# Attention output weights in two TensorE products a tile instead of three, with the output's low half stored beneath its high half

## What is computed

```
ln = layernorm(latents, ln_l_g, ln_l_b)
q = ln @ Wq.T
kv = jnp.concatenate([xn @ Wkv.T, ln @ Wlkv.T], axis=1)
...
attn = jax.nn.softmax(attn, axis=-1)
out = jnp.einsum('bhij,bhjd->bhid', attn, v)
out = out.transpose(0, 2, 1, 3).reshape(b, m, INNER)
return out @ Wo.T + bo
```

## Time and profile before

| | us |
|---|---|
| median of 3 runs | 823.86 (823.17 to 824.24) |
| the profiled execution | 826.39 |
| its span (first to last instruction) | 824.5 |
| PE busy | 760.7 (92%) |
| VectorE busy | 528.5 (64%) |
| ScalarE busy | 399.1 (48%) |
| GpSimd busy | 319.7 (39%) |

### The profile page before, as it was taken

The page is one execution under the profiler, slowest core; times in us unless marked ns, Lnnn a source line. Parts: engine busy times, 40 slices in busy tenths (PEclk is TensorE's granted clock), DMA queues, the critical chain, the costliest instruction groups (busy, mean ns, idle before and its releaser), DMA issues.

```text
span 824.5 us, 12845 instructions
## 1 busy us (share of the span) xinstructions
PE 760.7 (92%) x4881; PEld 621.4 (75%) x4881; DVE 528.5 (64%) x1163; ACT 399.1 (48%) x699; POOL 319.7 (39%) x281
## 2 busy tenths in 40 slices
PE   8889989999999999999999899983799999999996
PEld 7755546656755554679889888882788999999996
DVE  7767875773677683357455498975746656667552
ACT  3655634573465344563462244433034765557551
POOL 5502001200301022066361053334235878787783
PEclk9999999999999999999999999995699999999998
DMA  7000000000000100100030201121212444544532
GB/s 186 1 0 1 1 0 1 1 0 1 1 1 2 51 4 0 52 1 3 1 98 1 103 2 52 52 77 39 103 34 78 132 119 147 129 116 110 142 33 32
DMA packets 21509, 39.31 MB, mean 48 GB/s; under 512 B 4913, under 2 KB 16905, under 8 KB 19145
## 3 DMA queue, kind: packets, MB, share of 16 engines
q1 hardware_dynamic: 14793, 30.07, 11.1%
q0 software_dynamic: 6656, 8.43, 5.9%
HBM read 29.96 MB, written 8.40 MB: 47 GB/s over the span
## 4 chain that ended last, share of the span: by engine, by line
PE 56%; DVE 15%; ACT 4%; issue 3%; POOL 3%; another core or an unknown queue 0%; DVEq 0%; ACTq 0%
PE ps L481 18%; PE ps L650 8%; PE ps L1173 5%; PE ps L1176 5%; PE ps L754 5%; PE ps L671 2%; PE ps L672 2%; PE ps L612 2%; PE ps L475 1%; DVE sm L1613 1%; DVE rep L1807 1%; PE ps L1096 1%; DVE Pb L1617 1%; DVE sm L1622 1%; POOL out_dram L2724 1%
## 5 line engine op out<-in xcount | busy, mean ns | idle before, releaser
L650 PE MATMUL ps<-PT,VA 128*65 128x512 f32 (+1 forms) x288 | 147.5, 594 | 2.8 <-ACT PT L2116 2.5
L2116 ACT ACTIVATE PT<-ps 128x512 f32<-128x512 f32 x128 | 76.0, 594 | 62.0 <-PE ps L672 61.7
L481 PE MATMUL ps<-GT,wh 128*128 128x258 f32 (+1 forms) x768 | 94.6, 284 | 0.4 <-DVE GT L1905 0.4
L481 PEld LDWEIGHTS ps<-GT,wh 128*128 128x128 f32 x768 | 92.7, 189 | 0.6 <-DVE GT L1905 0.6
L2724 POOL DMA_INDIRECT out_dram<-ye,idx x40 | 67.2, 1679 | 19.9 <-issue 10.9
L2410 ACT ACTIVATE het<-ps,b1e 128x514 f32<-128x514 f32 x64 | 44.1, 689 | 61.4 <-PE ps L481 53.7
L1940 DVE TENSOR_TENSOR he<-het,he 128x514 fp32r<-128x514 f32 x64 | 45.6, 713 | 40.2 <-ACT he L1969 38.2
L671 PE MATMUL ps<-QA,KA 128*128 128x512 f32 x144 | 67.5, 468 | 0.8 <-ACT QB L1969 0.8
L2460 POOL TENSOR_TENSOR rs<-rs,half 128x4 f32<-128x4 f32 (+2 forms) x19 | 18.2, 956 | 123.5 <-DVE rs L1214 95.6
L612 PE MATMUL ps<-KA,QA 128*128 128x368 f32 x192 | 59.2, 414 | 4.4 <-DVE x L1422 2.1
L2602 POOL DMA_INDIRECT gt<-y_dram,idx x40 | 46.3, 1158 | 43.3 <-DVE gate L1895 33.5
(11 more groups left out here) (291 smaller groups left out, 1654.2 us busy)
## 6 DMA issues: line engine op xcount, KB each, us to landing
wr<-in_w1e_dram SPq DMA_DIRECT2D x8, 1024.0 KB, 5.0
wr<-in_w2e_dram SPq DMA_DIRECT2D x8, 1024.0 KB
x<-in_x_dram SPq DMA_DIRECT2D x4, 512.0 KB, 6.2
w<-in_w_dram SPq DMA_DIRECT2D x2, 1024.0 KB, 4.7
y_dram<-yr SPq DMA_DIRECT2D x3, 512.0 KB, 3.0
out_dram<-x SPq DMA_DIRECT2D x3, 512.0 KB, 4.1
b2r<-in_b2r_dram SPq DMA_DIRECT2D x8, 128.0 KB, 3.3
gt<-y_dram,idx POOLq DMA_INDIRECT x40
```

The lines of the kernel that those rows point to most:

```text
L481: op = pe.matmul(o, l, r, start=n == 0, stop=n == len(calls) - 1)
L650: pe.matmul(bank[6 + hf][0:65, :], VA[b][0:K, kt, h, :], PT[u % 4][0:K, :], start=kt == 0, stop=kt == 8).then_inc(p_pv, 1)
L2116: a.activation(PT[u % 4][0:K, :], bank[4 + u % 2][0:K, :], ACT.Exp, bias=0.0 if K == 128 else mcol[:, b:b + 1]).then_inc(a_exp, 1)
```

## The change

OT[0] gets 128 rows: rows 0 to 63 hold the output's high half, rows 64 to 127 its low half. wo[0] holds the high half of the weights in rows 0 to 63 and once more in rows 64 to 127, so that one matmul of 128 rows makes high by high and low by high. OT[1] is the companion: rows 0 to 63 the high half again, row 64 and row 65 the denominator's high half, row 96 its low half, zeros between; wo[1] holds the low half of the weights in rows 0 to 64 and the high row of bias and denominator in rows 65 and 96. Each tile then takes a matmul of 97 rows and one of 128.

For that, ScalarE makes two copies of a half instead of one and VectorE two subtractions instead of one; VA has two columns of ones; GpSimd clears 64 rows of wo[1] and of OT[1]; SyncE copies the rows of wo by three DMAs. The handling of a head's second half moves from its end to unit 0 of the next head, and `lnf` on GpSimd waits for VectorE's v_lr ahead of `add_row`.

```diff
-                three(bank[m][:, 0:258], [((OT[0][:, c], OT[1][:, c]), (wo[0][:, h, :], wo[1][:, h, :]))]).then_inc(p_wo, 1)
+                pe.matmul(bank[m][:, 0:258], OT[1][0:97, c], wo[1][0:97, h, :], start=True, stop=False)
+                pe.matmul(bank[m][:, 0:258], OT[0][:, c], wo[0][:, h, :], start=False, stop=True).then_inc(p_wo, 1)
...
             def attention(hi):
-                def ot(hf):
+                def ot(hi, hf):
                     qc = slice(512 * hf, 512 * hf + 512)
                     v.wait_ge(a_ot, 2 * hi + hf + 1)
-                    v.tensor_tensor(OT[1][:, qc], bank[6 + hf][0:65, :], f(OT[0][:, qc]), ALU.subtract).then_inc(v_ot, 1)
+                    v.tensor_tensor(OT[0][64:128, qc], bank[6 + hf][0:64, :], f(OT[0][0:64, qc]), ALU.subtract)
+                    v.tensor_tensor(OT[1][96:97, qc], bank[6 + hf][64:65, :], f(OT[1][64:65, qc]), ALU.subtract).then_inc(v_ot, 1)
...
+                    if hi and u == 0:
+                        ot(hi - 1, 1)
                     if hi and u % 2 and u < 16:
                         wo_tile(hi - 1, u // 2)
                     yield
-                ot(1)
+                if hi == 7:
+                    ot(hi, 1)
...
-                        a.wait_ge(g_wlo, 3)
-                    copy(OT[0][:, qc], bank[6 + hf][0:65, :]).then_inc(a_ot, 1)
+                        a.wait_ge(g_init, 7)
+                    copy(OT[0][0:64, qc], bank[6 + hf][0:64, :])
+                    copy(OT[1][0:66, qc], bank[6 + hf][0:66, :]).then_inc(a_ot, 1)
...
                     a.activation(PT[u % 4][0:K, :], bank[4 + u % 2][0:K, :], ACT.Exp,
                                  bias=0.0 if K == 128 else mcol[:, b:b + 1]).then_inc(a_exp, 1)
+                    if hi and u == 0:
+                        ot(hi - 1, 1)
                     if u == 9:
-                        ot(0)
+                        ot(hi, 0)
...
                 g_.wait_ge(v_z, 4 + g + 1)
+                if g % 2 == 0:
+                    g_.wait_ge(v_lr, g // 2 + 1)
                 add_row(g)
...
             low(wv[1], wv_in, wv[0], 2)
+            g_.wait_ge(g_wlo, 2)
+            step(g_.memset(f(wo[1][64:128, :, :]), 0.0))
+            settle()
             step(g_.memset(wo_in[:, :, 256:258], 0.0))
...
             low(wqk[1][:, :, 256:512], wqk_in[1], wqk[0][:, :, 256:512], 4)
+            g_.wait_ge(g_wlo, 4)
+            g_.memset(f(OT[1][64:128, :]), 0.0).then_inc(g_init, 1)
+            g_.wait_ge(g_init, 7)
             proj(1)
...
+            sp.wait_ge(g_wlo, 3)
+            for p in (65, 96):
+                sp.dma_start(f(wo[1][p:p + 1, :, :]), f(wo[0][64:65, :, :])).then_inc(d_rows, 16)
+            sp.wait_ge(d_rows, 96)
+            sp.dma_start(f(wo[0][64:128, :, :]), f(wo[0][0:64, :, :])).then_inc(d_rows, 16)
```

More of the change, by code:

```diff
@@ L162, in build @@
         wo_at = RA.at
-        wo = [RA(f"wo{i}", [65, H0, 258], F32R)[:, :, :] for i in range(2)]
+        wo = [RA(f"wo{i}", [128, H0, 258], F32R)[:, :, :] for i in range(2)]
         qa_at = RA.at
@@ L168, in build @@
         KB = RA("KB", [65, H0, NK], F32R)
-        VA = [RA(f"VA{i}", [128, 9, H0, 65]) for i in range(2)]
+        VA = [RA(f"VA{i}", [128, 9, H0, 66]) for i in range(2)]
         gg = RA("gg", [128, 3])
@@ L178, in build @@
         ot_at = RA.at
-        OT = [RA(f"OT{j}", [65, S], F32R) for j in range(2)]
+        OT = [RA(f"OT{j}", [128, S], F32R) for j in range(2)]
         wo_in = Arena(ot_at)("wo_in", [65, H0, 258])[:, :, :]
@@ L631, in wo_tile @@
                 if hi == 0 and qt == 0:
-                    pe.wait_ge(a_whi, 3)
                     pe.wait_ge(g_wlo, 3)
-                three(bank[m][:, 0:258], [((OT[0][:, c], OT[1][:, c]), (wo[0][:, h, :], wo[1][:, h, :]))]).then_inc(p_wo, 1)
+                    pe.wait_ge(d_rows, 112)
+                pe.matmul(bank[m][:, 0:258], OT[1][0:97, c], wo[1][0:97, h, :], start=True, stop=False)
+                pe.matmul(bank[m][:, 0:258], OT[0][:, c], wo[0][:, h, :], start=False, stop=True).then_inc(p_wo, 1)
                 busy[m] = (v_x, 8 * hi + qt + 1)
@@ L649, in pv @@
                         pe.wait_ge(a_vc, 2 * b + 2)
-                    pe.matmul(bank[6 + hf][0:65, :], VA[b][0:K, kt, h, :], PT[u % 4][0:K, :], start=kt == 0,
+                    pe.matmul(bank[6 + hf][0:66, :], VA[b][0:K, kt, h, :], PT[u % 4][0:K, :], start=kt == 0,
                               stop=kt == 8).then_inc(p_pv, 1)
@@ L2333, in scalar_program @@
             a.wait_ge(g_wo, 1)
-            halved(wo[0], wo_in, (d_rows, 64))
+            halved(wo[0][0:65, :, :], wo_in, (d_rows, 64))
             values(0, 2, 6)
@@ L2617, in gpsimd_program @@
             for va in VA:
-                g_.memset(va[:, :, :, 64:65], 1.0).then_inc(g_init, 1)
+                g_.memset(va[:, :, :, 64:66], 1.0).then_inc(g_init, 1)
             g_.wait_ge(g_init, 3)
@@ L2635, in gpsimd_program @@
             root_c(0)
-            low(wo[1], wo_in, wo[0], 3)
+            low(wo[1][0:65, :, :], wo_in, wo[0][0:65, :, :], 3)
             for i in range(2):
```

## The result

| | before | after |
|---|---|---|
| median | 823.51 | 834.68 |
| all executions | 822.88 to 824.24 | 833.60 to 834.94 |
| ratio | | 1.0137 (1.0122 to 1.0153) |
| the profiled execution | 826.39 | 833.60 |
| its span | 824.5 | 831.8 |

The account below looks back on a forecast made before the run. TensorE, busy 92% of the span, was taken as the bound. The terms -6.2 - 1.7 + 6.9 + 4.5 + 0.2 gave +3.7 us on 823.86, so 827.5 us, with a range of 821.0 to 831.5.

Parts of the forecast that it names:

- the two stall terms: Longer OT hand-overs in unit 9, +6.9 us, and at the borders of the heads, +4.5 us.
- products: Output tiles on TensorE: 192 matmuls become 128, and 52 of the 64 removed count at 0.119 us each, -6.2 us.
- clock: No term; a different clock granted at the start was named among what could overturn the sum.
- v_lr: Head 6: GpSimd's add to x waits for VectorE's L1466 and TensorE's gap goes, -1.7 us; bounds 0 and -2.1.
- unit 9: Second copy and subtraction lengthen the chain by 1.1 us, paid in six heads, 0.3 in head 7: +6.9; bounds +3.3, +8.
- the borders of the heads: Second half handled behind the next head's exp(0) and two reductions, so bank 7 and VectorE are late: +4.5; bounds 0, +8.
- the start: GpSimd's clearing of wo[1] rows stretches one VectorE cast, +0.2 us; bounds 0 and +1.0.
- A: Rival: TensorE's queued matmuls make good what the small engines lose, so products decide: -9.1, 814.8 us; chance 0.07.
- B: Rival: the one-row subtraction is nearly free, unit 9 costs 3.0 and borders 2.2: -2.3, 821.6 us; chance 0.10.
- C: Rival: the borders cost nothing, since exp(0) goes first and bank 7 has slack: -0.8, 823.1 us; chance 0.18.
- D: Rival: delays carry on as bank 2 passes on late, each of 11 places half as much again: +5.5, 833 us; chance 0.15.
- The cost of the second subtraction: In unit 9's chain on VectorE, one row by 512 was taken at 0.61 us; bounds 0.1 and 0.61.

Follow-up runs that it names:

- a_third: The changed kernel with the 97-row product of every output tile issued twice, 64 matmuls more; ratio to the kernel before 1.0197 (1.0175 to 1.0219).
- a_dma: The changed kernel with one copy and one subtraction a half, companion rows moved by SyncE's DMA, second half handled at the head's end; ratio to before 0.9919.
- b_1row: The kernel before plus a one-row subtraction of 512 behind each of the 16 subtractions, into a row nothing reads; ratio to before 1.0107 (1.0082 to 1.0131).
- b_copy2: The kernel before plus a second copy of 65x512 behind each of ScalarE's 16 copies, into a tile nothing reads; ratio to before 1.0038 (1.0023 to 1.0053).
- b_moved: The kernel before with only the second half's handling moved into the next head's unit 0; ratio to before 0.9999 (0.9985 to 1.0013).
- b_vlr: The kernel before with only GpSimd's wait for v_lr ahead of the two adds to x; ratio to before 0.9960 (0.9949 to 0.9972).

## Why the prediction was wrong, step by step

The change was 7.5 us dearer than forecast. The steps that failed are the two stall terms, too small by 1.6 and 2.3 us, the products, put 1.6 too high, and the clock, which had no term and came to 3.0.

| step | forecast | measured |
|---|---|---|
| products | -6.2 | -4.6 (a_third: -4.1, by the medians -4.9) |
| v_lr | -1.7 | -1.7 |
| unit 9 | +6.9 | +8.5 |
| the borders of the heads | +4.5 | +6.8 |
| the clock | 0 | +3.0 |
| the start | +0.2 | -0.6 |

The measured terms are of the traces and sum to 11.4, against 11.5 for the last output product. The two middle rows come from a_dma, which has the same products, the same wait for v_lr and falls of the clock at the same two places as the changed kernel, but the short chains and the old place. Between the two the starts of the scores drift apart only in the units in which OT changes hands; elsewhere they keep step to 0.03 us. Units 10 and 11 of head 6, in a_dma and in the changed kernel:

```profile
295.40 0.40 PE L674 MATMUL ps<-QA,KA 128*128 128x512 f32 x1
...
297.71 0.40 PE L674 MATMUL ps<-QA,KA 128*128 128x512 f32 x1
```

```profile
306.82 0.39 PE L672 MATMUL ps<-QA,KA 128*128 128x512 f32 x1
...
310.44 0.40 PE L672 MATMUL ps<-QA,KA 128*128 128x512 f32 x1
```

2.31 us and 3.62: the chain costs 1.3 there. Place by place, forecast and measured:

| head | 0 | 1 | 2 | 3 | 4 | 5 | 6 | 7 | sum |
|---|---|---|---|---|---|---|---|---|---|
| unit 9, forecast | 1.1 | 1.1 | 1.1 | 0 | 1.1 | 1.1 | 1.1 | 0.3 | 6.9 |
| unit 9, measured | 1.30 | 1.25 | 1.25 | 0.36 | 1.12 | 1.30 | 1.30 | 0.66 | 8.5 |
| border into this head, forecast | | 0.5 | 0.8 | 0.5 | 0 | 0.5 | 0.7 | 1.5 | 4.5 |
| border into this head, measured | | 0.78 | 1.15 | 0.81 | 0.16 | 0.84 | 1.14 | 1.90 | 6.8 |

Added alone to the kernel before, the second subtraction costs 7.5, the second copy 4.3 and the move 0.5, 12.3 together; the other 3.0 of these 15.3 come only when they stand together. L579's three waits of 0.83, 2.5 us, are of that kind, for they need the longer pair and the later place; neither b_1row, b_copy2 nor b_moved has them. The clock's 3.0 is the difference between two profiled executions, at 1.5 a fall. The kernel before is not free of such falls (b_vlr, the same up to head 6, had one at 149), so in the medians the clock's part may be smaller. The start is spread: head 0 begins between 38.1 and 39.2 in kernels that are nearly the same up to there, so the 0.2 forecast for the memset can be neither seen nor excluded.

- **Direction and mechanism**: right. One matmul of 0.12 us a tile is bought with two more instructions a half, and the chain of unit 9 is paid in full where the prediction said so, in heads 0, 1, 2, 4, 5 and 6. The 128 rows are free, the move gains nothing, v_lr gives its 1.7 in the traces, and the rivals are out: A by a_third and the longer waits, B by 690 ns for the single row, C by L579's 0.83 and the 6.8 at the borders, D because nothing is added between the places.
- **The cost of the second subtraction** was the first error in size: it made the chain 0.80 longer, not 0.61. The Trainium skill (VectorE: DVE Perf Modes, Two Vector instructions with no wait between them) says that an instruction whose input or output starts in another group of 32 partitions than the last one in the same memory is held until all earlier ones have finished. The trace agrees: the next instruction starts 0.70 and 0.72 after a subtraction that writes rows 64 to 127 or row 96, and 0.61 after the one that stays in its rows, here and in a_dma. The change made every one of these instructions such a one, and I costed them by the old pace. At the six places of 1.1 that is 0.9 us of the 1.6 by which unit 9 was short.
- **The borders and the covered places** were the second: I entered them by the waits that the trace of before showed, and took places without a wait as covered. In head 3's unit 9 (0 forecast) L612 now waits for x too, 0.4 us lost; in head 7's the output tile, 0.7 (0.3 forecast); L579 waits 0.83 instead of 0.5; the borders with L612 in unit 2 lost 1.15 instead of 0.8 and 0.7, the one from head 6 to head 7 1.9 instead of 1.5. Together the borders were 2.3 us short. A place that shows no wait is not thereby covered against a chain that grows by 1.3.
- **The products** were over-counted: by a_third 34 and by a_dma 39 of the 64 matmuls stand on the path, not 52. The waits that the change added can't be the whole reason, since a_dma doesn't have them; that I also counted matmuls ahead of waits that both kernels have is my reading, not tested.
- **The clock** was named only as what might overturn the sum, and for the start. Head 1's unit 10 (an idle of 1.80 in the earlier trace rows, busy 2.25 of 4 us) was nearly half empty already, and it fell there once 1.3 us more were added. That is 3.0 of the 7.5 us missed, if the medians lost as much as the profiled executions.
- **The range** ended at 831.5, since I gave D, delays that carry on, 0.15 and left half of it (833) out. What stood for the slow end was one mechanism at one price, and it is not what happened: between the places no delay grows. The bounds of the two stall terms, +8 each, would have reached 832.2, still short of 834.68: unit 9 alone came to 8.5, beyond its own bound, and the clock had no term.

## What to carry to other kernels

Here an instruction on one partition cost what one on 64 or 65 did (690 and 684 ns on VectorE), and in a chain that hands a buffer from engine to engine, its whole duration is paid: before splitting a copy or a subtraction in two, look who waits at its end, and whether a DMA can spread the result instead. To price a longer chain, count every place where it occurs, with the slack that each has, not only those that wait already. And in a stream that is dense on average, find the stretches of a few us in which TensorE mostly waits: here a little more waiting there came with half the clock behind them.
